# Attention's second score pass: the causal mask from coarse operand rows and GpSimd selects in place of mask matmuls

## The chip, the core and the metric

The kernel runs on one core of a Trainium2 chip. The metric is the device time of one execution in microseconds. A core has five engines: TensorE (PE; PEld is its weight load), VectorE (DVE), ScalarE (ACT), GpSimd (POOL) and SyncE (SP), which work in parallel, each in its own order, and wait for one another by semaphores. SyncE and ScalarE issue DMAs on hardware queues, GpSimd on a software one.

## The reference, cut to what matters

A two-layer transformer piece: causal attention with ALiBi, an expert-choice feed-forward layer, a gated scan mixer and a token-choice expert layer. The change lies in the first:

```python
x = x + _L0_attn_ref(_layernorm(x), W_attn, W_proj)   # x: 16 batches x 512 tokens x 128
# inside: H = 16 heads of D = 8
scores = einsum('bhqd,bhkd->bhqk', q, k) / sqrt(D)
bias   = where(k_pos <= q_pos, slope_h * (k_pos - q_pos), -inf)
att    = softmax(scores + bias, axis=-1)
y      = einsum('bhqk,bhkd->bhqd', att, v)
```

Every score with a key later than its query must add nothing to the softmax.

## The kernel before

**Attention** (function `attention`) takes the first 827 us. Its work is cut into 16 batches of 4 units; a unit is 4 heads of one batch. The scores are made twice. The first pass (S, lines 309 to 321) has queries on partitions and is only there for the row maxima, which VectorE reduces from PSUM (line 425). The second pass (E, lines 322 to 339) has keys on partitions and queries along the row; the maximum is already subtracted in it by two operand rows, and ScalarE takes the exponential (line 486) into `probs`. The products with V (line 344) sum over keys on TensorE.

Both passes contract over operand tiles `qop` and `kop` ([128, 16 heads, 512], bf16), of which there are two sets that alternate by batch. Rows 0 to 47 hold bf16 parts of q and k, rows 48 to 50 the ALiBi terms, rows 96 and 97 the maxima; all other rows are zero. S reads rows 0 to 95, E all 128. The constant rows are loaded once per set by `constant_rows` on SyncE, when VectorE has cleared the set (`s_init`); `s_rows[n]` counts them, and TensorE waits for it before a batch's first S.

**The mask.** A tile j of 128 keys needs the queries from 128 j on, and only its diagonal block of 128 x 128 holds pairs to be masked. Before each group of score matmuls a matmul of the identity with a constant tile of 0 and -1e30 writes this block: `maskq` in S (line 316), `maskk` in E:

```python
pe.matmul(out[:, :, 0:P], identb[:], maskk[:, 0:per, :], start=True, stop=False, ...)   # L332
for a in range(per):
    mm = pe.matmul(out[:, a, :], kop[...], qop[...], start=False, ...)                   # L335
```

A unit has 11 of these in E: eight of 128 columns, two of 256, one of 512.

**The order.** `ORDER` lists the pieces of a step by hand: S0 to S10 of unit u, E0 to E5 of unit u - 2, M (the maxima turned to rows), V0 and V1 of unit u - 2, V2 and V3 of unit u - 3. Four steps (st = 0 to 3) make a batch. SyncE writes the maximum rows into `qop` (line 194, two DMAs a unit); E0 waits for them.

**The next batch's operands** are made in between: statistics and normalisation on VectorE in step 0, x transposed after S5 of step 0, q projected at the end of step 0, k after S4 of step 1 and v at the end of step 2. For q and k in turn ScalarE takes the high part, VectorE the rest (line 395), GpSimd the middle and low parts (lines 257, 259) and sends them to DRAM (line 231); when both have landed, `place` on GpSimd issues six DMAs (lines 242, 244) that bring them back as operand rows. The next batch's S0 waits for these (`s_op`).

Of the kernel before, what the change touches and what calls it, by code (L numbers as in the profile page):

```python
# [14 lines left out]
BF16 = mybir.dt.bfloat16  # L15
# [3 lines left out]
ALU = mybir.AluOpType  # L19
# [3 lines left out]
P = 128  # L23
C = 128
T = 512
NB = 16
TT = T // P
# [4 lines left out]
H = 16  # L32
D = C // H
G = 4
HG = H // G

TERMS = [(0, 0), (1, 0), (2, 0), (0, 1), (1, 1), (0, 2)]
ROW_ALIBI = 8 * len(TERMS)
ROW_MAX = 96
# [21 lines left out]
def attention(nc, x_all, ident, x_in, w_attnT, qkv_scr, y_scr, rec_scr, shared, c_ident, c_identb, c_maskq, c_maskk, c_rows, nb=NB):  # L61


    with ExitStack() as ctx:
        def sb(name, shape, dt):
            return ctx.enter_context(nc.sbuf_tensor(name, shape, dt))

        def sem(name):
            return ctx.enter_context(nc.semaphore(name))
# [8 lines left out]
        maskk = sb("maskk", [P, HG, P], BF16)  # L78
# [43 lines left out]
        s_ex = sem("exp_done")  # L122
        s_pv = sem("pv_done")
# [3 lines left out]
        EN = 6  # L127
# [46 lines left out]
        def _(sp):  # L174
            for dst, src in ((x_all[:, 0:2 * TT, :], x_in[:, 0:2 * TT, :]), (ident[:], c_ident), (identb[:], c_identb),
                             (maskq[:], c_maskq), (maskk[:], c_maskk),
                             (wT[:], w_attnT.rearrange("c (s f) -> c s f", s=3))):
                sp.dma_start(dst, src).then_inc(s_first, 16)
            def constant_rows(n):
                sp.wait_ge(s_init[n], 2)  # L180
                for dst, a, b in ((kop[n][ROW_ALIBI:ROW_ALIBI + 3], 0, 3), (qop[n][ROW_ALIBI:ROW_ALIBI + 3], 3, 6),
                                  (kop[n][ROW_MAX:ROW_MAX + 2], 6, 8)):
                    sp.dma_start(dst.rearrange("p h q -> p (h q)"), c_rows[a:b]).then_inc(s_rows[n], 16)

# [30 lines left out]
        def _(pool):  # L215
# [32 lines left out]
            def prepare(n, b, first=False):  # L248
# [3 lines left out]
                if first:  # L252
                    clear_v(0)
                for s in range(2):

                    pool.wait_ge(s_mf, s + 2 if first else MISC0 + MISC * (b - 1) + 2 * s + 2)
                    pool.tensor_tensor(parts[s][:, 1], rest[:], zeros[:], ALU.add).then_inc(s_mid, 1)  # L257
                    pool.wait_ge(s_mid, 2 * b + s + 1)
                    pool.tensor_tensor(parts[s][:, 2], rest[:], parts[s][:, 1], ALU.subtract).then_inc(s_lo, 1)
                    keep_part(n, b, s)  # L260
                if b == 1:
                    pool.wait_ge(s_init[1], 2)
                place(n, b)

            prepare(0, 0, True)
            clear_v(1)
            for b in range(1, nb):
                prepare(b % 2, b)

        @block.tensor  # L270
        def _(pe):
            pe.wait_ge(s_first, 96)
# [24 lines left out]
            def step(n, b, st, last):  # L297
# [4 lines left out]
                    if st == 0 and there(G * b):  # L302
                        pe.wait_ge(s_op, 16 * 6 * (b + 1))
                        pe.wait_ge(s_rows[n], 48)
                    for what in ORDER:
# [16 lines left out]
                        if what[0] == "E" and there(u_exp):  # L322
                            j, h0, nh = e_units[k]
                            u = k
                            bank = psE[u % 2]
                            if k == 0:
                                pe.wait_ge(s_mrow, 32 * (u_exp + 1))
                            per = nh // 2 if j < 3 else 4
                            pe.wait_ge(s_ex, EN * u_exp + u)
                            for h in range(0, nh, per):  # L330
                                out = bank[:, h // per, 0:per * W[j]].rearrange("p (h q) -> p h q", h=per)
                                pe.matmul(out[:, :, 0:P], identb[:], maskk[:, 0:per, :], start=True, stop=False, skip_group_check=True)  # L332
                                for a in range(per):
                                    hh = HG * e + h0 + h + a
                                    mm = pe.matmul(out[:, a, :], kop[m][:, hh, P * j:P * j + P], qop[m][:, hh, P * j:T],  # L335
                                                   start=False, stop=(a == per - 1), skip_group_check=True)
                            mm.then_inc(s_er, 1)
                        u_v, m_v, e_v = (u_exp, m, e) if k < 2 else (u_exp - 1, m_old, e_old)
                        if what[0] == "V" and there(u_v):
                            pe.wait_ge(s_ex, 1 + EN * u_v + [2, 4, 5, 6][k])  # L340
# [22 lines left out]
        def _(dve):  # L363
# [22 lines left out]
            dve.wait_ge(s_first, 96)  # L386
# [1500 lines left out]
def two_blocks_kernel(nc, x, wattnT, wprojT, rw, rb, w1, b1, w2, b2, win, wout, prm, rows, gwT, rmsw, W1T, W2T, W3T, cst, out):  # L1887
# [13 lines left out]
    with ExitStack() as keep:  # L1901
# [5 lines left out]
        with ExitStack() as ctx:  # L1907
# [11 lines left out]
                      cst["c_maskq"], cst["c_maskk"], cst["c_rows"], nb)  # L1919
# [21 lines left out]
def constants(nt, bf16):  # L1941
# [8 lines left out]
    for _ in range(3):  # L1950
# [3 lines left out]
    rows += [np.ones((H, T), bf16)] * 3 + [-np.ones((H, T), bf16)] * 2  # L1954
    digits = np.array([[4.0 ** (7 - k) * j for j in (1, 1, 2, 3)] + [4.0 ** (7 - k) * 3 - 0.5] for k in range(9)])
    return dict(
        c_ident=np.eye(P, dtype=np.float32), c_identb=np.eye(P, dtype=np.float32).astype(bf16),
        c_maskq=wide(below[:, None], (P, HG, P), bf16), c_maskk=wide(below.T[:, None], (P, HG, P), bf16),
# [52 lines left out]
```

## Time and profile before

| | us |
|---|---|
| median of 3 runs | 1905.36 |
| the runs | 1899.95 to 1909.52 |
| the profiled execution | 1911.37 |
| its span | 1909.6 |
| TensorE, VectorE, ScalarE, GpSimd busy | 1386.0, 1278.0, 739.0, 817.9 |

All rows come from the profiled execution; their times count from the start of its span. "Busy" is the union of an engine's instructions. A matmul's duration includes its way through the array, so what one costs in a dense row of them is the distance between starts.

### The profile page before, as it was taken

To read this page: it belongs to the slowest core of one execution; us is meant where nothing else is said; L and a number is where in the kernel's file an instruction comes from. 1 tells how busy PE (TensorE), PEld (TensorE's weight loads), DVE (VectorE), ACT (ScalarE), POOL (GpSimd) and SP (SyncE) were. 2 spreads that over 40 slices of the span, in tenths; PEclk is the share of its full clock that TensorE was granted. 3 is DMA by queue.
4 is the path that set the end of the run, shared out by engine and by line. 5 is a ranking of instruction groups with operands and counts; after the bars stand their busy time and mean duration, and the time that the engine had idled before them with its cause. 6 is when DMAs were issued, how large, how long until landed. Compare 5 with 4: busy or idle time off the path is not lost. (4 is left out here: it accounts for less than half of the span.)

```text
span 1909.6 us, 33952 instructions
## 1 busy us (share of the span) xinstructions
PE 1386.0 (73%) x9370; PEld 869.1 (46%) x9371; DVE 1278.0 (67%) x3736; ACT 739.0 (39%) x1489; POOL 817.9 (43%) x716
## 2 busy tenths in 40 slices
PE   1788889889888988949315254541809999999996
PEld 0355445555555545438204222221806556555654
DVE  4667667667677766738671189998686666666664
ACT  0255445445555555511212132222424444444443
POOL 3222222222222222024006546565616888888886
PEclk9999899999999999965557765565559999999999
DMA  3533333233233233136104300030032333333332
GB/s 76 133 73 71 63 74 80 64 75 81 74 74 72 72 72 74 39 125 220 43 0 112 63 30 22 16 112 6 22 163 38 41 43 42 42 41 43 41 42 35
DMA packets 72986, 124.48 MB, mean 65 GB/s; under 512 B 17888, under 2 KB 42272, under 8 KB 70480
## 3 DMA queue, kind: packets, MB, share of 16 engines
q0 software_dynamic: 39168, 59.42, 18.6%
q1 hardware_dynamic: 25728, 51.42, 8.3%
q10 hardware_dynamic: 8032, 12.93, 1.9%
q8 instruction: 28, 0.46, 0.1%
q14 instruction: 30, 0.25, 0.1%
HBM read 65.25 MB, written 57.94 MB: 65 GB/s over the span
## 5 line engine op out<-in xcount | busy, mean ns | idle before, releaser
L425 DVE TENSOR_REDUCE mx<-psS 128x1 f32<-128x384 f32 (+3 forms) x704 | 428.2, 638 | 222.5 <-PE psS L319 211.9
L486 ACT ACTIVATE probs<-psE 128x1024 f32<-128x1024 f32 (+2 forms) x384 | 326.7, 884 | 290.3 <-PE psE L335 289.2
L316 PE MATMUL psS<-maskq,identb 128*128 128x128 bf16 (+2 forms) x704 | 178.5, 254 | 109.4 <-DMA kop<-qkv_scr 88.3
L1804 POOL DMA_INDIRECT out<-ex_y,ex_idx x144 | 235.8, 1638 | 48.6 <-issue 42.6
L319 PE MATMUL psS<-kop,qop 96*128 96x128 bf16 (+3 forms) x1024 | 246.5, 309 | 0.0
L335 PE MATMUL psE<-qop,kop 128*128 128x512 bf16 (+3 forms) x1024 | 231.4, 307 | 0.0
L332 PE MATMUL psE<-maskk,identb 128*128 128x128 bf16 (+2 forms) x704 | 175.0, 249 | 2.5 <-ACT probs L486 2.5
L344 PE MATMUL psY<-probs,vaug 128*32 128x512 f32 (+3 forms) x2048 | 176.5, 455 | 0.0
L1795 POOL DMA_INDIRECT ex_xg<-expert_tab,ex_idx x144 | 141.8, 985 | 66.2 <-issue 42.1
L316 PEld LDWEIGHTS psS<-maskq,identb 128*128 128x128 bf16 x704 | 67.8, 98 | 204.2 <-DVE mx L425 81.7
L1778 DVE SCALAR_TENSOR_TENSOR ex_h<-ex_psG,ex_w,ex_up 128x352 f32<-128x352 f32 x144 | 84.1, 584 | 109.9 <-ACT ex_w L1879 107.7
L257 POOL TENSOR_TENSOR parts<-rest,zeros 128x512 bf16<-128x512 f32 x32 | 40.7, 1272 | 261.7 <-DVE rest L395 261.5
L1862 PE MATMUL ex_psY<-ah_w3s,ex_hT 128*128 (+1 forms) x864 | 133.1, 290 | 0.7 <-ACT ex_hT L1873 0.7
L335 PEld LDWEIGHTS psE<-qop,kop 128*128 128x128 bf16 x1024 | 95.8, 99 | 59.3 <-issue 9.7
L251 POOL TENSOR_TENSOR rstd<-veps,mhalf 128x4 f32<-128x4 f32 x16 | 16.6, 1036 | 243.0 <-DVE veps L374 243.0
L1862 PEld LDWEIGHTS ex_psY<-ah_w3s,ex_hT 128*128 128x128 f32 (+1 forms) x864 | 107.7, 191 | 20.7 <-issue 2.7
L319 PEld LDWEIGHTS psS<-kop,qop 96*128 96x128 bf16 x1024 | 98.7, 101 | 36.0 <-issue 5.0
L1844 PE MATMUL ex_psU<-ah_w1s,ex_xT 128*128 x288 | 110.4, 465 | 0.5 <-ACT ex_xT L1883 0.5
L1845 PE MATMUL ex_psG<-ah_w2s,ex_xT 128*128 x288 | 109.8, 463 | 0.0
L1872 ACT ACTIVATE ex_hT<-ex_psH 128x256 f32<-128x256 f32 x144 | 55.2, 383 | 135.2 <-PE ex_psH L1838 135.2
L344 PEld LDWEIGHTS psY<-probs,vaug 128*32 128x32 f32 x2048 | 71.2, 114 | 59.7 <-issue 36.7
L1222 PE MATMUL mx_psO<-mx_wout,mx_z 128*128 128x128 f32 x128 | 33.0, 440 | 86.1 <-DVE mx_z L1362 86.1
(309 smaller groups left out, 2669.9 us busy)
## 6 DMA issues: line engine op xcount, KB each, us to landing
y_scr<-ysb SPq DMA_DIRECT2D x64, 256.0 KB, 2.2
qkv_scr<-parts POOLq DMA_DIRECT2D x32, 384.0 KB, 3.4
qop<-qkv_scr POOLq DMA_DIRECT2D x16, 384.0 KB, 5.8
kop<-qkv_scr POOLq DMA_DIRECT2D x16, 384.0 KB, 6.5
expert_tab<-table_rows SPq DMA_DIRECT2D x1, 4352.0 KB, 14.5
qop<-qkv_scr POOLq DMA_DIRECT2D x16, 256.0 KB, 7.2
kop<-qkv_scr POOLq DMA_DIRECT2D x16, 256.0 KB, 8.3
pj_num<-y_scr SPq DMA_DIRECT2D x16, 256.0 KB
```

What stands on the lines that cost most here:

```text
L316: pe.matmul(out[:, :, P * j:w], identb[:], maskq[:, 0:nh, :], start=True, stop=False, skip_group_check=True)
L319: mm = pe.matmul(out[:, h, :], qop[n][0:96, hh, P * j:P * j + P], kop[n][0:96, hh, 0:w], start=False, stop=(h == nh - 1), skip_group_check ...
L332: pe.matmul(out[:, :, 0:P], identb[:], maskk[:, 0:per, :], start=True, stop=False, skip_group_check=True)
L335: mm = pe.matmul(out[:, a, :], kop[m][:, hh, P * j:P * j + P], qop[m][:, hh, P * j:T], start=False, stop=(a == per - 1), skip_group_check= ...
L344: mm = pe.matmul(psY[32 * h:32 * h + 32, P * k:T], vaug[m_v][:, k, HG * e_v + h, :], probs[e_v % 2][k][:, h, :], start=(k == 0), stop=(k = ...
L425: dve.tensor_reduce(mx[:, j, h0:h0 + nh], psS[u % 2][:, 0:nh * w].rearrange("p (h k) -> p h k", h=nh), AX, ALU.max).then_inc(s_su, 1)
L486: act.activation(dst, src, ACT.Exp).then_inc(s_ex, 1)
L1795: pool.indirect_dma_start(xg[t % 4][:], None, ytab, bass.IndirectOffsetOnAxis(ap=idx[t % 8][:], axis=0))\
L1804: pool.indirect_dma_start(out, bass.IndirectOffsetOnAxis(ap=idx[t % 8][:], axis=0), y[m][:], None, compute_op=ALU.add).then_inc(s_sc[m], 16)
L1844: pe.matmul(psU[n][:, 0:DE], xT[n][:], flat(w1s[:, e, :]), start=True, stop=True).then_inc(s_g2, 1)
L1845: pe.matmul(psG[n][:, 0:DE], xT[n][:], flat(w2s[:, e, :]), start=True, stop=True).then_inc(s_g, 1)
L1862: i = pe.matmul(psY[:, 0:C], hT[m][0:wd, f], flat(w3s[0:wd, f, e, :]), start=(f == 0), stop=(f == len(FC) - 1))
```

## The change

The E pass no longer has its mask matmuls: the first score matmul of a bank has `start=True` itself. The mask comes in two parts. A coarse one is put into rows 51 to 81 of both operand sets, one row for each boundary between blocks of 16 positions: the `kop` row is 1 for keys in block i, the `qop` row -1e30 for queries in blocks before i. They work in both passes, and the S pass keeps `maskq` beside them. What is left, keys later than the query within the same block of 16, GpSimd sets to zero after the exponential, with one `affine_select` on the diagonal block of each `probs` tile: four a unit, 128 partitions x 4 heads x 128. The V matmuls wait for the selects (`s_msk`) and no longer for the exponential. GpSimd's work is written out anew, so that its selects stand among the preparation of the next batch. The 31 rows of each tile are loaded by one more DMA each on SyncE.

```diff
+ROW_SUB = ROW_ALIBI + 3
+SUB = 16
+NSUB = T // SUB - 1
...
-        maskk = sb("maskk", [P, HG, P], BF16)
...
+                for dst, a in ((kop[n], 0), (qop[n], NSUB)):
+                    sp.dma_start(dst[ROW_SUB:ROW_SUB + NSUB], c_subs[a:a + NSUB].unsqueeze(1).to_broadcast([NSUB, H, T]))\
+                        .then_inc(s_rows[n], 16)
...
+            def clear_future(u, j):
+                if 0 <= u < G * nb:
+                    pool.wait_ge(s_ex, 1 + EN * u + (2, 4, 5, 6)[j])
+                    block_ = probs[u % 2][j][:, :, 0:P]
+                    pool.affine_select(block_, block_, [[0, HG], [1, P]], ALU.is_ge, 0.0, base=0, channel_multiplier=-1).then_inc(s_msk, 1)
...
+            for b in range(nb + 1):
+                more = b + 1 < nb
+                for st in range(G if b < nb else 2):
+                    u = G * b + st - 2
+                    if st == 0 and more:
+                        factors(b + 1)
+                    if st == 1 and more:
+                        split_rest(b + 1, 0)
+                    if st == 2 and more:
+                        if b == 0:
+                            pool.wait_ge(s_init[1], 2)
+                        place(1 - b % 2, b + 1)
+                    for j in range(2):
+                        clear_future(u, j)
+                    if st == 1 and more:
+                        split_rest(b + 1, 1)
+                    for j in range(2, TT):
+                        clear_future(u, j)
...
-                        pe.wait_ge(s_rows[n], 48)
+                        pe.wait_ge(s_rows[n], 80)
...
-                                pe.matmul(out[:, :, 0:P], identb[:], maskk[:, 0:per, :], start=True, stop=False, skip_group_check=True)
...
-                                                   start=False, stop=(a == per - 1), skip_group_check=True)
+                                                   start=(a == 0), stop=(a == per - 1), skip_group_check=True)
...
-                            pe.wait_ge(s_ex, 1 + EN * u_v + [2, 4, 5, 6][k])
+                            pe.wait_ge(s_msk, TT * u_v + k + 1)
...
+    sub_of, sub = np.arange(T) // SUB, 1 + np.arange(NSUB)[:, None]
+    subs = np.concatenate([sub_of == sub, np.where(sub_of < sub, -1e30, 0.0)])
```

`factors` is the `rstd` power of line 251, `split_rest` lines 256 to 260 for q (s = 0) or k (s = 1).

SyncE's queue at the start, from the first constant rows to the first maximum rows. Before (names: tile written <- source, rows x elements):

```order
L183 DMA kop<-c_rows 3x8192
L183 DMA qop<-c_rows 3x8192
L183 DMA kop<-c_rows 2x8192
L183 DMA kop<-c_rows 3x8192
L183 DMA qop<-c_rows 3x8192
L183 DMA kop<-c_rows 2x8192
L194 DMA qop<-mT 1x4x512 x6
```

and now:

```order
L186 DMA kop<-c_rows 3x8192
L186 DMA qop<-c_rows 3x8192
L186 DMA kop<-c_rows 2x8192
L188 DMA kop<-c_subs 31x16x512
L188 DMA qop<-c_subs 31x16x512
L186 DMA kop<-c_rows 3x8192
L186 DMA qop<-c_rows 3x8192
L186 DMA kop<-c_rows 2x8192
L188 DMA kop<-c_subs 31x16x512
L188 DMA qop<-c_subs 31x16x512
L200 DMA qop<-mT 1x4x512 x6
```

In each set, two DMAs of 31 rows x 16 heads x 512 stand behind the three small ones, and set 1's stand ahead of the first maximum rows.

TensorE in a step, from E2 to S5 (psE is E's PSUM tile, psS is S's). Before:

```order
L332 MATMUL psE<-maskk,identb 128x128
L335 MATMUL psE<-qop,kop 128x384
L332 MATMUL psE<-maskk,identb 128x128
L335 MATMUL psE<-qop,kop 128x384
L316 MATMUL psS<-maskq,identb 128x128
L319 MATMUL psS<-kop,qop 128x384
L332 MATMUL psE<-maskk,identb 128x128
L335 MATMUL psE<-qop,kop 128x384
L332 MATMUL psE<-maskk,identb 128x128
L335 MATMUL psE<-qop,kop 128x384
L316 MATMUL psS<-maskq,identb 128x128
L319 MATMUL psS<-kop,qop 128x384
```

and now:

```order
L363 MATMUL psE<-qop,kop 128x384 x2
L345 MATMUL psS<-maskq,identb 128x128
L348 MATMUL psS<-kop,qop 128x384
L363 MATMUL psE<-qop,kop 128x384 x2
L345 MATMUL psS<-maskq,identb 128x128
L348 MATMUL psS<-kop,qop 128x384
```

The matmuls of `maskk` are gone; nothing else has moved.

GpSimd while it prepares a batch. Before, from `rstd` into the six operand DMAs (parts: the three parts of q or k; qkv_scr: their copy in DRAM):

```order
L251 TENSOR_TENSOR rstd<-veps,mhalf 128x4
L257 TENSOR_TENSOR parts<-rest,zeros 128x512
L259 TENSOR_TENSOR parts<-rest,parts 128x512
L231 DMA qkv_scr<-parts 128x3x512
L257 TENSOR_TENSOR parts<-rest,zeros 128x512
L259 TENSOR_TENSOR parts<-rest,parts 128x512
L231 DMA qkv_scr<-parts 128x3x512
L242 DMA qop<-qkv_scr 24x8192
L244 DMA kop<-qkv_scr 24x1x8192
```

and now, the part of steps 1 and 2 of a batch:

```order
L262 TENSOR_TENSOR parts<-rest,zeros 128x512
L264 TENSOR_TENSOR parts<-rest,parts 128x512
L237 DMA qkv_scr<-parts 128x3x512
L272 AFFINE_SELECT probs_0<-probs_0 128x4x128
L272 AFFINE_SELECT probs_1<-probs_1 128x4x128
L262 TENSOR_TENSOR parts<-rest,zeros 128x512
L264 TENSOR_TENSOR parts<-rest,parts 128x512
L237 DMA qkv_scr<-parts 128x3x512
L272 AFFINE_SELECT probs_2<-probs_2 128x4x128
L272 AFFINE_SELECT probs_3<-probs_3 128x512
L248 DMA qop<-qkv_scr 24x8192
L250 DMA kop<-qkv_scr 24x1x8192
```

Two selects now stand between the splitting of q and of k, two between k's DMA to DRAM and the operand DMAs, and the next unit's selects behind those.

## Rows read from the trace of the kernel before

**Rows 1.** Busy time by windows: attention's batches 1 to 14, then batch 15 and the end.
```profile
99.20:762.20 663.00, 591.65 (x5265) 337.82 (x5266) 462.72 (x998) 337.43 (x448) 149.61 (x181) 0.95 0.32 73
762.20:827.00 64.80, 52.93 (x498) 28.24 (x498) 36.42 (x58) 33.32 (x43) 0.10 (x1) 0.95 0.16 52
```

**Rows 2.** Timeline, TensorE: first score matmul of batches 1, 8 and 9 (start, us).
```profile
99.22 0.61 PE L316 MATMUL psS<-maskq,identb 128*128 128x512 bf16 x1 [8.97 <-DMA kop<-qkv_scr]
...
434.85 0.39 PE L316 MATMUL psS<-maskq,identb 128*128 128x512 bf16 x1 [1.20 <-DMA kop<-qkv_scr]
...
482.05 0.39 PE L316 MATMUL psS<-maskq,identb 128*128 128x512 bf16 x1 [4.09 <-DMA kop<-qkv_scr]
```

**Rows 3.** Timeline, TensorE, one step: mask matmuls (L332) and what follows each.
```profile
450.55 0.22 PE L332 MATMUL psE<-maskk,identb 128*128 128x128 bf16 x1
450.61 0.32 PE L335 MATMUL psE<-qop,kop 128*128 128x384 bf16 x1
...
453.25 0.27 PE L332 MATMUL psE<-maskk,identb 128*128 128x256 bf16 x1
453.36 0.38 PE L335 MATMUL psE<-qop,kop 128*128 128x256 bf16 x2
...
454.18 0.38 PE L332 MATMUL psE<-maskk,identb 128*128 128x512 bf16 x1
454.40 0.39 PE L335 MATMUL psE<-qop,kop 128*128 128x128 bf16 x4
```

**Rows 4.** Timeline, TensorE: S4 of the same batch's step 0; V2 and V3 of step 2.
```profile
440.46 0.23 PE L316 MATMUL psS<-maskq,identb 128*128 128x128 bf16 x1 [1.11 <-DVE mx L425]
...
459.66 0.81 PE L344 MATMUL psY<-probs,vaug 128*32 128x256 f32 x13
```

**Rows 5.** Timeline, GpSimd: preparing batch 9's operands during batch 8.
```profile
448.50 1.28 POOL L257 TENSOR_TENSOR parts<-rest,zeros 128x512 bf16<-128x512 f32 x1 [10.18 <-DVE rest L395]
...
451.58 0.82 POOL L231 DMA_DIRECT2D qkv_scr<-parts  x1 [0.57 <-POOL parts L259]
454.94 1.27 POOL L257 TENSOR_TENSOR parts<-rest,zeros 128x512 bf16<-128x512 f32 x1 [2.54 <-DVE rest L395]
...
457.74 0.79 POOL L231 DMA_DIRECT2D qkv_scr<-parts  x1 [0.30 <-POOL parts L259]
461.03 0.55 POOL L242 DMA_DIRECT2D qop<-qkv_scr  x1 [2.50 <-DMA qkv_scr<-parts]
```

**Rows 6.** Timeline, ScalarE: exponentials of E3 in that step 1.
```profile
453.06 0.81 ACT L486 ACTIVATE probs<-psE 128x768 f32<-128x768 f32 x1
```

**Rows 7.** Groups by form, GpSimd (last two numbers before the bar: busy us, mean ns).
```profile
L257 POOL TENSOR_TENSOR parts<-rest,zeros 128x512 bf16<-128x512 f32 x32 | 40.7, 1272 | 261.7 <-DVE rest L395 261.5
...
L1449 POOL TENSOR_TENSOR gt_scaled<-x_all,gt_acc_a 128x512 f32<-128x512 f32 x8 | 8.3, 1039 | 0.6
...
L217 POOL MEMSET zeros<- 128x512 f32 x1 | 0.5, 527 | 0.0
```

**Rows 8.** Timeline, SyncE: the constant rows of operand set 0.
```profile
9.44 0.32 SPq L183 DMA_DIRECT2D kop<-c_rows  x1
9.80 0.24 SPq L183 DMA_DIRECT2D qop<-c_rows  x1
```

**Rows 9.** DMA view, 9.3 to 16 us in 40 slices, and SyncE's queue (packets, MB, share).
```profile
GB/s 0 0 0 0 0 0 293 0 0 0 0 0 294 0 0 0 0 0 0 0 0 0 0 196 0 0 0 0 0 0 0 0 0 0 0 0 0 0 0 0
...
q1 hardware_dynamic: 16, 0.13, 10.5%
```

**Rows 10.** DMA view, 822.1 to 824.1 us: SyncE's queue under the projection's loads.
```profile
q1 hardware_dynamic: 159, 0.29, 48.0%
```

**Rows 11.** DMA view, 394.9 to 396.1 us: SyncE's queue, two DMAs of maximum rows.
```profile
q1 hardware_dynamic: 16, 0.01, 2.3%
```

**Rows 12.** Timeline, TensorE, batch 0: its first score matmul; first exponent matmul of unit 0.
```profile
51.24 0.61 PE L316 MATMUL psS<-maskq,identb 128*128 128x512 bf16 x1 [25.62 <-DMA kop<-qkv_scr]
...
71.80 0.38 PE L335 MATMUL psE<-qop,kop 128*128 128x512 bf16 x1
```

More of the change, by code:

```diff
@@ L58, in kept_sums, with attention @@
     return y_scr[lo:hi, :, D, :]
-def attention(nc, x_all, ident, x_in, w_attnT, qkv_scr, y_scr, rec_scr, shared, c_ident, c_identb, c_maskq, c_maskk, c_rows, nb=NB):
+def attention(nc, x_all, ident, x_in, w_attnT, qkv_scr, y_scr, rec_scr, shared, c_ident, c_identb, c_maskq, c_rows, c_subs, nb=NB):
     with ExitStack() as ctx:
@@ L122, in attention @@
         s_ex = sem("exp_done")
+        s_msk = sem("future_cleared")
         s_pv = sem("pv_done")
@@ L175, in _ @@
             for dst, src in ((x_all[:, 0:2 * TT, :], x_in[:, 0:2 * TT, :]), (ident[:], c_ident), (identb[:], c_identb),
-                             (maskq[:], c_maskq), (maskk[:], c_maskk),
+                             (maskq[:], c_maskq),
                              (wT[:], w_attnT.rearrange("c (s f) -> c s f", s=3))):
@@ L246, in place, with factors @@
                     row += w
-            def prepare(n, b, first=False):
+            def factors(b):
                 pool.wait_ge(s_xn, b)
@@ L251, in prepare @@
                 pool.tensor_tensor(rstd[:], veps[:], mhalf[:], ALU.pow).then_inc(s_rstd, 1)
[L252 to L265, printed above, removed]
-            clear_v(1)
-            for b in range(1, nb):
-                prepare(b % 2, b)
+            def split_rest(b, s):
+                pool.wait_ge(s_mf, MISC0 + MISC * (b - 1) + 2 * s + 2 if b else s + 2)
+                pool.tensor_tensor(parts[s][:, 1], rest[:], zeros[:], ALU.add).then_inc(s_mid, 1)
+                pool.wait_ge(s_mid, 2 * b + s + 1)
+                pool.tensor_tensor(parts[s][:, 2], rest[:], parts[s][:, 1], ALU.subtract).then_inc(s_lo, 1)
+                keep_part(b % 2, b, s)
@@ new lines, in clear_future @@
+            def clear_future(u, j):
[3 more added lines that the diff above has]
+                    pool.affine_select(block_, block_, [[0, HG], [1, P]], ALU.is_ge, 0.0, base=0, channel_multiplier=-1).then_inc(s_msk, 1)
+            factors(0)
+            clear_v(0)
+            for s in range(2):
+                split_rest(0, s)
+            place(0, 0)
+            clear_v(1)
@@ L270, in _ @@
         @block.tensor
         def _(pe):
-            pe.wait_ge(s_first, 96)
+            pe.wait_ge(s_first, 80)
             def x_transposes(b, use):
@@ L385, in _ @@
             dve.memset(kop[0][:].bitcast(F32), 0.0).then_inc(s_init[0], 1)
-            dve.wait_ge(s_first, 96)
+            dve.wait_ge(s_first, 80)
             norm_stats(0)
@@ L1918, in two_blocks_kernel @@
             attention(nc, x_all, ident, x, wattnT, qkv_scr, y_scr, rec_scr, shared, cst["c_ident"], cst["c_identb"],
[L1919 removed]
+                      cst["c_maskq"], cst["c_rows"], cst["c_subs"], nb)
             project(nc, x_all, y_scr, rec_scr, shared, wprojT, x_scr, rw, rb, norm_tab, score_tab, scores, ident, nb)
@@ L1957, in constants @@
         c_ident=np.eye(P, dtype=np.float32), c_identb=np.eye(P, dtype=np.float32).astype(bf16),
-        c_maskq=wide(below[:, None], (P, HG, P), bf16), c_maskk=wide(below.T[:, None], (P, HG, P), bf16),
+        c_maskq=wide(below[:, None], (P, HG, P), bf16),
+        c_subs=subs.astype(bf16),
         c_rows=np.stack(rows).reshape(8, H * T),
```

## The prediction

> **What bounds the kernel now.** I read the windows first. Batches 1 to 14 of attention take 663.0 us, 47.4 us each, with TensorE busy for 591.65 us of them [rows 1]. So TensorE looks like the bound, and mask matmuls taken from it look like time won. The timeline says otherwise. Every batch opens with TensorE idle for its operand rows to come back from DRAM: 15 such waits after batch 0's, from 1.20 to 8.97 us [rows 2]. A batch is therefore a loop: first score matmul, k's projection in step 1, the split on VectorE and GpSimd, a round trip through DRAM, the next first score matmul. What TensorE saves between k's projection and the batch's end only lengthens the wait. The third thing to read is the start of the kernel, where SyncE loads the constant rows [rows 8, 9], for the change puts four large DMAs there.
>
> **What the change removes.** In a dense row of matmuls, the one behind a mask matmul starts 0.06 us after it for 128 columns, 0.11 for 256 and 0.22 for 512 [rows 3]. A unit has 8, 2 and 1 of them: 0.48 + 0.22 + 0.22 = 0.92 us, or 59 us for 64 units. Of this only what lies on the loop counts. In step 0, S4 waits 1.11 us for VectorE [rows 4], which normalises the next batch there; what E0 to E3 save ahead of or near it is lost in this wait but for some 0.06 us. E4 and E5 behind it give 0.44. In step 1 the masks of E0 to E3 stand ahead of S6, behind which VectorE splits k: 8 x 0.06 = 0.48. Together 1.0 us a batch. The other 2.6 us of a batch's four units go into the wait for the operands (4.09 us in batch 9 [rows 2]).
>
> **What it adds on GpSimd.** Four selects a unit, 512 elements a partition, in and out of SBUF. The trace has no select. Below, the nearest row is a memset of this size, 0.53 us, which only writes; above, the two-input addition, 1.27 us; another two-input product takes 1.04 [rows 7]. I take 1.0 us: one input, but a comparison with it. The Trainium skill (GPSIMD Engine Reference, Performance pitfalls for Q7 kernels) gives compare-and-select bodies 1.03 to 2.03 cycles an element, from which I estimate 0.44 to 0.87 us at its 1.2 GHz; no row here shows it, and it would leave the sum as it is.
>
> Where they stand in the queue matters more. In step 1, q's DMA to DRAM is issued until 452.40 us, k's split began at 454.94, and E3's exponential ended at 453.87 [rows 5, 6]. The select of probs_0 fits in at 452.4. That of probs_1 must wait for E3's exponential and ends at about 454.9: k's split starts 0.1 us late at 1.0 us a select, 0.3 at 1.27. The next two selects stand between k's DMA to DRAM (done at 458.53) and the operand DMAs (461.03), where GpSimd waited 2.50 us for the landing [rows 5]: two selects fit up to 1.25 us each. V2 and V3 of the next step stood at 459.66 [rows 4]; their selects end at about 460.6, so TensorE stalls for some 1 us there, and again before V0, since the six operand DMAs (3.3 us) go first. These stalls come after k's projection; the wait for the operands hides them, with 4.09 + 2.6 us of cover. If that cover were gone, they would cost some 2 us a batch. ScalarE and VectorE issue what they did.
>
> So a batch gains 1.0 - 0.1 = 0.9 us, 14 of them 12.6. Batch 15 has no operands to wait for: 4 x 0.92 = 3.7 us, less two selects (2.0) behind the last exponential: 1.7. Sum of the steady part: **-14 us**. The clock there was 0.95 of full [rows 1]; the waits stay about as long, so I leave it alone.
>
> **What it adds at the start.** Each of the four new DMAs carries 31 rows x 16 KB = 508 KB, in pieces of 1 KB. Which engines carry it decides the case. The small DMAs of 3, 3 and 2 rows were issued within 0.7 us [rows 8], but their bytes stand in three separate slices, at 10.3, 11.3 and 13.2 us, with nothing else moving [rows 9]: each row went to an engine of its own, and the next DMA's rows queued on the same engines, in order. The projection's loads, whose outermost dimension is 8, kept 48.0% of 16 engines busy, at most eight [rows 10]. The number of engines follows the outermost dimension; 31 has no divisor up to 16 but 1, and I take **one engine**. The Trainium skill (DMA: Bandwidth & Descriptors, Why a DMA increments its semaphore by 16 and not by 1) says this outright: the largest count up to 16 that divides the slowest dimension of both sides, on the lowest-numbered engines. By that rule 31 rows go to one engine, and the trace agrees for 3 rows and for 8.
>
> An engine's rate: 0.29 MB in 0.480 x 16 x 2.0 = 15.4 engine-us is 19 GB/s with 2 KB packets [rows 10]; 8 KB in 0.023 x 16 x 1.2 = 0.44 engine-us is 19 GB/s with 1 KB packets [rows 11]. The lower bound is 0.13 MB in 0.105 x 16 x 6.7 = 11.3 engine-us, 11.5 GB/s [rows 9]. I take 19, since those packets are the nearest in size: 26.7 us a DMA. Set 0's two start at about 14.4 us (13.2 plus a row) and set 1's follow on the same engine, ahead of unit 0's maximum rows, which share that queue. Four make 107 us. I add 10 us for this engine's sixteenth of the operand rows of batches 0 and 1 (2 x 1.5 MB / 16 at 19 GB/s). The queue is empty at 131 us.
>
> Three waits follow. S0 of batch 0, at 51.24 us [rows 12], needs set 0's rows, at about 73. E0 of unit 0, at 71.80 [rows 12], needs the maximum rows: 131. Batch 1's S0 needs set 1's rows: 131 too. The second rules: from 71.80 to TensorE's arrival at batch 1 (99.22 - 8.97 = 90.25 [rows 2]) it had 18.4 us of work, now 16.6 without the masks of two units, and arrives at 148. Batch 1's operands have landed by then, its 8.97 us of waiting are used up, and the cost is 148 - 99 = **+49 us**. The mask tile that is no longer loaded saves nothing, as the clearing of the operand sets outlasts it.
>
> **Sum.** 49 - 14 = +35. The profiled execution took 1911.37 us (span 1909.6), which gives 1946; it stands 6.0 us above the median, and from the median 1905.36 the time is **1940 us**.
>
> **Rivals.**
> - A, the forecast: 1940. With 22 GB/s (packets without their gaps) the queue is empty at about 115: 1924; some more traffic on the engine: 1955. Chance 0.57.
> - B, the 31 rows are spread over many engines. Four times 0.5 MB are then in before 51.24 us, as the 0.29 MB of [rows 10] were within 2 us on eight engines. Nothing is left at the start but the -14: 1905 - 14 = 1891, faster. It decides as soon as set 0's rows land by 51 us and set 1's by 70, which three engines do. For it speaks that the loads in the trace with few rows had 16 or fewer; against it the separate slices of [rows 9]. [...] Chance 0.14.
> - C, one engine, but the maximum rows do not queue behind. Then batch 1's S0 waits for set 1's rows alone: 131 - 99 = +32, less 14: 1923. Chance 0.10.
> - D, selects of 2 us (GpSimd's software being slow, as nothing here excludes): k's split starts 1.5 us late, the operand DMAs another 1.5, so each batch grows by 2 us instead of shrinking: +28, the end 0, the start +49: 1982. The gain is gone at about 1.5 us a select. Chance 0.13.
> - E, one engine at 11.5 GB/s: 44 us a DMA, queue empty at 207, start +125: 2016. Chance 0.06.
>
> **The numbers.** The range 1903 to 1985 holds A, C and D and leaves out B and E, 0.20; A's own range is 1920 to 1960. A measurement of this kernel tells about 0.5%, 9.5 us, from no change: 1896 to 1915. Faster comes from B (0.12); the same from what is left of B (0.02) and the low ends of A and C (0.04 each): 0.10; slower is the rest, 0.78.
>
> **What would show it.** At the start: E0 of unit 0 at 110 to 150 us instead of 71.80, waiting for a DMA; S0 of batch 0 at 65 to 80; long stretches with a DMA share of 1/16. From batch 1 to 15: 46.5 us a batch instead of 47.4; waits for kop<-qkv_scr still at every batch start; k's split within 0.3 us of the exponential-plus-select; selects of 0.8 to 1.3 us; TensorE waiting about 1 us for GpSimd in step 2 and hardly elsewhere. It is wrong if E0 of unit 0 stands near 70 us (then B), if GpSimd is busy through the batch (D), or if the operand waits vanish, for then the 59 us were all to be had.

## The result and the profile after

The change makes the kernel slower: 1963.31 us (median of four runs, 1961.09 to 1974.93) against 1907.44 us for the kernel before (four runs, 1899.95 to 1911.22), a ratio of 1.031 with a 95% interval of 1.026 to 1.036. That lies inside the forecast's range of 1903 to 1985, 23 us above its 1940 and 3 above the 1960 at which the range of its case A ended. The profiled execution took 1962.95 us, its span is 1961.2 us and its mean granted clock 0.835, against 1909.6 us and 0.842 before.

The windows of the changed kernel, cut as in [rows 1] at the first score matmul (S0) of batch 1 and of batch 15 (window, length, then busy us and count of TensorE, its weight load, VectorE, ScalarE and GpSimd, granted clock, DMA share, GB/s); the second window ends at the projection's first matmul:

```profile
166.20:817.80 651.60, 547.74 (x4649) 289.29 (x4650) 472.59 (x1011) 336.02 (x448) 289.70 (x406) 0.96 0.33 74
817.80:886.30 68.50, 48.05 (x433) 23.21 (x433) 36.14 (x58) 33.32 (x43) 16.30 (x26) 0.90 0.18 57
```

Batches 1 to 14 take 651.6 us, 11 less than the 663.0 of [rows 1]. TensorE's busy time fell by 44 us there, so three quarters of what it saved became idle time. From S0 of batch 15 to the projection's first matmul it is 68.5 us where the same stretch took 70.6 before. Both are gains. The loss is all ahead of the first window, which begins 67 us later than before (99.22 in [rows 2]). The timeline of TensorE there, with the start of batch 0, of unit 0's exponents and of batch 1:

```profile
75.77 0.59 PE L345 MATMUL psS<-maskq,identb 128*128 128x512 bf16 x1 [50.08 <-issue]
...
146.28 1.03 PE L363 MATMUL psE<-qop,kop 128*128 128x512 bf16 x2 [49.88 <-DMA qop<-mT]
...
166.19 0.38 PE L345 MATMUL psS<-maskq,identb 128*128 128x512 bf16 x1 [0.60 <-DVE mx L453]
```

S0 of batch 0 is 24.5 us later than in [rows 12], E0 of unit 0 waits 49.88 us for its maximum rows and is 74.5 us later, and batch 1 starts without waiting for operands. SyncE's own queue shows why the maximum rows are late (start, duration of the issue):

```profile
10.46 0.26 SPq L188 DMA_DIRECT2D kop<-c_subs  x1
10.75 22.78 SPq L188 DMA_DIRECT2D qop<-c_subs  x1
33.58 36.38 SPq L186 DMA_DIRECT2D kop<-c_rows  x1
...
70.61 0.26 SPq L188 DMA_DIRECT2D kop<-c_subs  x1
70.91 45.72 SPq L188 DMA_DIRECT2D qop<-c_subs  x1
116.68 24.15 SPq L200 DMA_DIRECT2D qop<-mT  x2
```

DMA issues that otherwise take about 0.26 us take 22.78, 36.38 and 45.72 us behind the 31-row loads, and SyncE issues nothing meanwhile. (With 32-row loads, in e1 below, the issues of `qop<-c_subs` take 0.49 us each.) The DMA view says how fast they go. First SyncE's queue from 56 to 67 us, when nothing else moves, and from 55 to 75 us, then from 33.6 to 53 us, while batch 0's operand rows are loaded, then from 86 to 118 us, while x and batch 1's operand rows are (packets, MB, share of 16 engines):

```profile
q1 hardware_dynamic: 246, 0.25, 6.8%
...
q1 hardware_dynamic: 457, 0.54, 8.5%
...
q1 hardware_dynamic: 114, 0.12, 3.4%
...
q1 hardware_dynamic: 227, 0.23, 3.2%
```

A share of 6.8% is about one engine of 16 (the 8.5% hold the small rows of set 1 too). Where nothing else moves, the view shows 22 to 26 GB/s in slice after slice, 23 on average, which is 45 ns for a piece of 1 KB. Under other traffic 0.12 MB take 19.4 us and 0.23 MB take 32, some 6 to 7 GB/s. The 1984 pieces of the four loads need 89 us undisturbed; they ran from 14.6 to 145.4 us, 42 us longer.

In the steady part, the waits of TensorE from 100 to 750 us (what waits for what: us in total, times, longest), before:

```profile
PE psS L316 <- DMA kop<-qkv_scr: 49.9, 13, 6.6
PE psS L316 <- DVE mx L425: 8.2, 15, 1.1
PE psM L355 <- DVE rest L395: 2.5, 14, 0.2
```

and after:

```profile
PE psE L363 <- DMA qop<-mT: 59.3, 7, 49.9
PE psS L345 <- DMA kop<-qkv_scr: 44.2, 11, 7.7
PE psS L345 <- DVE mx L453: 24.1, 66, 1.6
PE psY L372 <- POOL probs L272: 4.5, 13, 1.0
```

The operand waits are still there, as the forecast said; VectorE is now waited for 66 times in place of 15; the selects cost few direct waits. One wait is new and was not foreseen: apart from the 49.9 us at the start, E0 waits six times later on, up to 2.71 us, for maximum rows, where before no such wait stands in the list. It goes with the selects: it is 12.0 us in e1 below and 0.2 in e4, which leaves them out. The groups by form give a select's price (busy us, mean ns), which no row of before had:

```profile
L272 POOL TENSOR_SCALAR_AFFINE_SELECT probs<-probs 128x512 f32<-128x512 f32 x256 | 158.5, 639 | 320.0 <-ACT probs L514 319.6
```

It is 0.64 us. GpSimd's timeline during batch 2, against [rows 5]:

```profile
232.29 0.63 POOL L272 TENSOR_SCALAR_AFFINE_SELECT probs<-probs 128x512 f32<-128x512 f32 x1 [0.73 <-ACT probs L514]
233.18 1.28 POOL L262 TENSOR_TENSOR parts<-rest,zeros 128x512 bf16<-128x512 f32 x1 [0.25 <-DVE rest L423]
...
236.79 1.22 POOL L272 TENSOR_SCALAR_AFFINE_SELECT probs<-probs 128x512 f32<-128x512 f32 x2
239.28 0.56 POOL L248 DMA_DIRECT2D qop<-qkv_scr  x1 [1.26 <-DMA qkv_scr<-parts]
```

k's split waits 0.25 us for VectorE's remainder and not for the select ahead of it. The next two selects fit into the wait for the landing, of which 1.26 us are left.

### The profile page after: what moved, and what is told of

It is laid out like the page before. It is cut to its first block and busy times, and to the rows that moved or that the text cites. A ratio compares the mean times of both kernels' runs of the same rounds, so it can differ in the third digit from the quotient of the medians.

```text
span 1961.2 us, 32900 instructions
## 1 busy us (share of the span) xinstructions
PE 1336.4 (68%) x8666; PEld 813.4 (41%) x8667; DVE 1283.6 (65%) x3736; ACT 737.7 (38%) x1489; POOL 976.9 (50%) x972
## 3 DMA queue, kind: packets, MB, share of 16 engines
q0 software_dynamic: 39168, 59.42, 17.9%
## 5 line engine op out<-in xcount | busy, mean ns | idle before, releaser
L272 POOL TENSOR_SCALAR_AFFINE_SELECT probs<-probs 128x512 f32<-128x512 f32 x256 | 158.5, 639 | 320.0 <-ACT probs L514 319.6
L363 PE MATMUL psE<-qop,kop 128*128 128x512 bf16 (+3 forms) x1024 | 212.7, 311 | 62.5 <-DMA qop<-mT 59.3
L363 PEld LDWEIGHTS psE<-qop,kop 128*128 128x128 bf16 x1024 | 89.8, 99 | 111.1 <-DMA qop<-mT 50.2
L1208 POOL TENSOR_TENSOR mx_rstd<-mx_nrm_veps,mx_mhalf 128x8 f32<-128x8 f32 (+1 forms) x19 | 40.7, 2142 | 92.9 <-DVE mx_nrm_veps L595 84.0
```

Of the source, the lines that this page charges most:

```text
L272: pool.affine_select(block_, block_, [[0, HG], [1, P]], ALU.is_ge, 0.0, base=0, channel_multiplier=-1).then_inc(s_msk, 1)
```

## The experiments

Each was timed beside the kernel before, in five sessions: e1, e2, e4 and e5 (its median there 1907.47 us), e3 and e6 (1908.83), e7 and e8 (1903.61), e9 and e10 (1910.62), e11 (1905.78). Between sessions a difference of a few us says nothing. A window or a step length comes from one execution of each kernel. "Batches 1 to 14" is S0 of batch 1 to S0 of batch 15 in the profiled execution. In e1, e3, e4, e5, e7, e8 and e9 a 32nd coarse row of zeros goes with the 31, which changes no score.

### e1: 32 rows in place of 31

```
+ NROW = NSUB + 1
- dst[ROW_SUB:ROW_SUB + NSUB], c_subs[a:a + NSUB].unsqueeze(1).to_broadcast([NSUB, H, T])
+ dst[ROW_SUB:ROW_SUB + NROW], c_subs[a:a + NROW].unsqueeze(1).to_broadcast([NROW, H, T])
```

> The changed kernel with a 32nd coarse row of zeros, so that each new load has an outermost dimension of 32 instead of 31. Theory (31 rows run on one DMA engine, and set 1's rows and the maximum rows queue there): the queue at the start is gone, S0 of batch 0 near 51 us, E0 of unit 0 near 72 instead of 146, S0 of batch 1 near 99 instead of 166, time 1963 - 67 = 1896 us (1888 to 1902). Rival (the 2 MB themselves cost, however they are spread): E0 of unit 0 after 100 us, time above 1925.

Measured 1904.84 us, ratio 0.9995 (0.9971 to 1.0018). S0 of batch 0 is at 53.91 us, E0 of unit 0 at 74.36, and batch 1's first score matmul at 102.07, 2.5 us later than before (99.61) in place of 67. One row more takes 58 us off. From 10 to 20 us, while set 0's two loads are under way, SyncE's queue shows

```profile
q1 hardware_dynamic: 1060, 1.17, 71.0%
```

against the 6.8% of the change: the 32 rows are spread over most of the 16 engines. The start is settled: the cost is that 31 rows go one piece after another. The time is 3 us above the range given, because the gain of the steady part was half of what was expected: batches 1 to 14 took 656.9 us, 6.0 less than before.

### e2: the kernel before with the four loads alone

```
+ for dst, a in ((kop[n], 0), (qop[n], NSUB)):
+     sp.dma_start(dst[ROW_SUB:ROW_SUB + NSUB], c_subs[a:a + NSUB]...).then_inc(s_rows[n], 16)
- pe.wait_ge(s_rows[n], 48)
+ pe.wait_ge(s_rows[n], 80)
```

> The kernel before, with its mask matmuls, plus only the four 31-row loads. Theory: the whole start cost comes without the rest of the change: E0 of unit 0 near 146 us, time 1907 + 67 = 1974 us (1966 to 1981). Rival (the start is late because of GpSimd's new order or the missing mask tile): 1905 to 1915 us.

Measured 1978.07 us, ratio 1.0351 (1.0326 to 1.0375). Without any of the change's compute the four loads cost 70.6 us; the rest of the change is then worth 1978.07 - 1963.31 = 14.8 us, the 14 of the forecast's sum.

### e3: 31 rows for operand set 0, 32 for set 1

```
+ m = NROW if n else NSUB
```

> The change, with the coarse rows of operand set 0 loaded as 31 rows (on one DMA engine) and those of set 1 as 32 rows, the last one zero (on all). Theory (four loads on one engine's ring, in order; the second set is only late because it stands behind the first there, and because 16 KB operand rows and 1 KB rows take turns on that engine): the first S0 stays where the change has it, at 75 to 77 us; the wait for the maximum rows before the first E0 (49.88 us in the change) goes nearly away, so the first E0 is at 95 to 105 us and S0 of batch 1 at 115 to 125 us in place of 166.19. The total is 1911 to 1925 us, 38 to 52 below the change. Rival (what is late is SP's own queue, whatever the second set does): the first E0 stays behind 130 us and the total over 1945 us.

Measured 1932.54 us, ratio 1.012 (1.0068 to 1.0172), 31 below the change and 8 above the range given. The mechanism is the theory's: no wait for the maximum rows stands in TensorE's waits there, E0 of unit 0 is at 100.78 us in place of 146.28 and S0 of batch 1 at 127.73 in place of 166.19. But S0 of batch 0 is at 79.78 us, 3 later than the theory had it, and S0 of batch 1 is 3 later too. Part of that is given back in batches 1 to 14, which took 659.0 us. Set 0's loads are worth 1932.54 - 1904.84 = 28 us, set 1's the other 31.

### e4: e1 without the selects

```
- if 0 <= u < G * nb:                      + if False:
- pe.wait_ge(s_msk, TT * u_v + k + 1)      + pe.wait_ge(s_ex, 1 + EN * u_v + [2, 4, 5, 6][k])
```

> e1 without the 256 selects; the V matmuls wait for the exponentials again, and keys later than the query within a block of 16 stay in the sums (left out: that part of the mask). Theory (the selects lie in GpSimd's gaps and under the operand waits): within 5 us of e1, 1 to 2 us of that at attention's end. Rival (the selects delay k's split or the operand DMAs in each batch, or V on TensorE on the loop): 10 us or more faster than e1.

Measured 1899.03 us, ratio 0.9954 (0.9936 to 0.9972). The 256 selects cost 5.8 us here by the medians and 6.7 in batches 1 to 14, just over the 5 expected at most and well under the rival's 10; the two ratios' intervals touch. Batches 1 to 14 took 650.2 us: the masks' 59 us of TensorE are worth 12.7 us of the loop (forecast: 14 x 1.0). Its operand waits grew to 83.4 us from 100 to 750 us, where e1 has 55.1: that is where the rest of the saved time stands.

### e5 and e6: the operand rows in another order, with and without mask matmuls

```
- qkv_scr[n, 0, 0:k].rearrange("a (d h) q -> (a d) (h q)", d=D)
+ qkv_scr[n, 0, 0:k].rearrange("a (d h) q -> d a (h q)", d=D)
- k_src.unsqueeze(0).to_broadcast([k, D, H * T])
+ k_src.unsqueeze(1).to_broadcast([D, k, H * T])
```

e5 is e1 with this edit; e6 is the kernel before, its mask matmuls kept, with it.

> e1 with the operand rows in another order, d outermost and the part inside it, so that each of the six operand DMAs has an outermost dimension of 8, where kop's had 3 and 2. Theory (a batch is a loop through the operand round trip, whose last landing is set by the few engines of kop's DMAs): the operand waits of some 4 us a batch shrink to under 1, batch period 46.5 to 43.5 us, time 1896 - 14 x 3 = 1854 us (1845 to 1870). Rival (the round trip is bound by bytes or by the written partitions): landing unchanged, 1890 to 1900 us.

> The kernel before, mask matmuls kept, with only the order of the operand rows in the six operand transfers changed (outermost dimension of 8 in place of 2 and 3). Theory (before, each batch is a loop through the operand rows' transfer, and without that wait the steps are set by TensorE and VectorE together, so that the mask matmuls are only partly paid): batches 1 to 14 fall from 662.9 us to about 625 to 645 us (e5, without mask matmuls: 616.9), and the total is 1863 to 1888 us. Rival 1 (the mask matmuls cost their whole 0.92 us a unit once the wait is gone, 3.7 us a batch): batches 1 to 14 take 669 us or more, the total is 1905 to 1916 us, and the new order alone is worth nothing. Rival 2 (VectorE sets the steps, the mask matmuls are free): within 5 us of e5, 1852 to 1862 us.

e5 took 1857.09 us, ratio 0.9732 (0.9712 to 0.9752); e6 took 1854.67 us, ratio 0.9719 (0.967 to 0.9769). The wait that bounded each batch is gone in both. From 380 to 470 us, the last two operand transfers of each batch land (bytes, median us to landing) in e1 after

```profile
qop<-qkv_scr POOLq DMA_DIRECT2D x2, 128.0 KB, 15.6
kop<-qkv_scr POOLq DMA_DIRECT2D x2, 128.0 KB, 17.9
```

and in e5 after

```profile
qop<-qkv_scr POOLq DMA_DIRECT2D x2, 128.0 KB, 12.0
kop<-qkv_scr POOLq DMA_DIRECT2D x2, 128.0 KB, 13.1
```

The five microseconds between 17.9 and 13.1 are about what S0 waited for. The second result is the surprise: with the loop gone, the whole change (e5) is no faster than the kernel before with the same edit (e6). My theory (masks partly paid) and the rival (masks wholly paid) for e6 both fell, and its rival 2, within 5 us of e5, came out in the number. Its reason did not; e7 shows that.

### e7: e5 without the selects

The edit is that of e4.

> e5 (the change with a 32nd zero coarse row and with the operand rows in the new order) without GpSimd's selects; the output leaves out the mask inside the 16x16 blocks on the diagonal. Theory: with no operand wait in the loop, a step is set by VectorE's reductions and TensorE together; of e5's waits only those for POOL (7.3 us in 650) and part of those for the maximum rows hang on the selects, so the total falls by 3 to 8 us, to 1849 to 1854 us. Rival (the selects also slow VectorE, and so every step, since its hi/lo subtraction is 307 ns in e5 and 175 ns in e6, and its scalar operation 390 against 328): VectorE's groups go back to their times of before and the total falls by 10 to 20 us, to 1837 to 1847 us.

Measured 1826.39 us, ratio 0.9592 (0.957 to 0.9613): 31 us below e5 and 28 below e6, in other sessions; by the ratios it is 27 and 24, and the profiles have the projection's first matmul 29.3 and 31.1 us earlier. So selects and mask matmuls cost some 24 to 31 us each here; that they are equal is chance. Neither the theory nor the rival had it so large. The windows over batches 1 to 14 of e5, e6 and e7, in this order:

```profile
93.60:710.40 616.80, 536.35 (x4592) 284.70 (x4648) 471.35 (x1009) 339.97 (x448) 292.49 (x406) 0.98 0.37 79
```
```profile
90.20:709.30 619.10, 572.80 (x5181) 325.74 (x5264) 460.51 (x1002) 339.60 (x448) 152.46 (x182) 0.99 0.37 78
```
```profile
92.60:682.00 589.40, 532.11 (x4650) 283.70 (x4649) 458.44 (x996) 338.64 (x448) 152.23 (x182) 0.99 0.39 82
```

e5 and e7 run the same matmuls; e5 needs 27.4 us more for its 14 batches, 2.0 a batch. Three things are seen. VectorE is 12.9 us busier. TensorE waits 7.3 us for GpSimd from 100 to 700 us and 3.0 for maximum rows, neither of which e7 has; e7 in turn waits 7.9 us for operand rows again, in six short waits. And the granted clock is 0.98 in place of 0.99. Here is VectorE's subtraction for the maximum rows beside GpSimd's selects in e5:

```profile
338.24 0.69 DVE L464 TENSOR_TENSOR mhl<-mx,mhl 128x16 bf16<-128x16 f32 x1
```
```profile
338.24 1.22 POOL L273 TENSOR_SCALAR_AFFINE_SELECT probs<-probs 128x512 f32<-128x512 f32 x2
```

and the same step in e7:

```profile
325.48 0.18 DVE L464 TENSOR_TENSOR mhl<-mx,mhl 128x16 bf16<-128x16 f32 x1
```

0.69 us in place of 0.18, at the head of the chain that leads to the maximum rows. Over 100 to 700 us its mean is 307 ns in e5 and 175 in e7. The Trainium skill (SBUF — State Buffer, SBUF: two separate sides) says that a VectorE operation with two SBUF inputs and a GpSimd operation that reads SBUF exclude each other for a whole instruction; these rows agree. The normalising scalar operation (`xn`) takes 387 ns in e5 and 328 in e7; no run shows why.

The clock falls in step 0, behind a wait of the same length in both. e5:

```profile
319.40 0.29 PE L346 MATMUL psS<-maskq,identb 128*128 128x128 bf16 x1 [1.22 <-DVE mx L454]
319.48 0.53 PE L349 MATMUL psS<-kop,qop 96*128 96x384 bf16 x1
319.80 0.85 PE L364 MATMUL psE<-qop,kop 128*128 128x384 bf16 x2
```

e7:

```profile
308.17 0.23 PE L346 MATMUL psS<-maskq,identb 128*128 128x128 bf16 x1 [1.22 <-DVE mx L454]
308.24 0.33 PE L349 MATMUL psS<-kop,qop 96*128 96x384 bf16 x1
308.40 0.49 PE L364 MATMUL psE<-qop,kop 128*128 128x384 bf16 x2
```

The same matmuls take 0.53 and 0.85 us at the lower level (1.2 GHz, granted clock 0.53 from 319.40 to 322.80 us) and 0.33 and 0.49 at the higher one. The falls can be counted by the windows of step 0. Batches 8 and 9 of e5:

```profile
401.89:415.60 13.71, 11.61 (x84) 6.12 (x85) 9.97 (x29) 6.27 (x8) 3.54 (x5) 0.88 0.05 20
447.13:459.12 11.99, 10.00 (x84) 5.19 (x85) 10.30 (x29) 6.16 (x8) 3.67 (x5) 1.00 0.06 23
```

In nine of e5's 14 batches the clock falls and step 0 takes 13.47 to 13.73 us; in the other five it takes 11.78 to 12.11: 1.6 us a fall. e7 has four. e11 below runs the same matmuls and selects as e5 and has four falls as well: its batches 1 to 14 take 609.9 us, 7.0 less than e5's and 20.5 more than e7's. So of the 27.4 us some 7 go with the clock and some 20 with the selects. What makes it fall in one batch and not in the next is not shown.

### e8: e5 with the mask matmuls back in step 0

```
+ if st == 0:
+     pe.matmul(out[:, :, 0:P], identb[:], maskk[:, 0:per, :], start=True, stop=False, ...)
- start=(a == 0)
+ start=(a == 0 and st > 0)
```

> e5 with the kernel before's mask matmuls put back in step 0 of each batch alone (the step in which VectorE also makes the next batch's norms, and in which the granted clock of e5 falls to the lower level for some 3.5 us after TensorE's waits for VectorE; in e6, with all mask matmuls, it does not fall). Theory (without mask matmuls TensorE idles enough in step 0 to lose its clock, which gives back what their leaving saves): the granted clock of 100 to 700 us rises from 0.97 to 0.99 or 1.00, batches 1 to 14 fall from 616.9 to 590 to 608 us, and the total is 1835 to 1848 us, below both e5 and e6. Rival (VectorE sets the steps whatever TensorE does): the total is within 4 us of e5, 1853 to 1861 us, even where the clock rises.

Measured 1856.81 us, ratio 0.975 (0.9728 to 0.9771): as e5. The rival held: step 0 took 13.04 us, e5's 13.03, and batches 1 to 14 took 622.2 us. Its reason did not: the clock falls in five batches in place of e5's nine, some 6 us less by 1.6 a fall (an estimate), and where it holds, step 0 takes 12.3 to 13.0 us where e5's takes 11.8 to 12.1. So the equal time hides two changes that about cancel: what the clock gave back, the mask matmuls cost. The expectation's remark that in e6 the clock does not fall was wrong too: it falls there in batches 1 and 8.

### e9: selects in step 3 alone, mask matmuls in steps 0 to 2

```
+ if st != 3:
+     pe.matmul(out[:, :, 0:P], identb[:], maskk[:, 0:per, :], start=True, stop=False, ...)
+ for j in range(2 if st == 3 else 0): clear_future(u, j)
+ for j in range(2, TT if st == 3 else 2): clear_future(u, j)
```

> The mask matmuls of the kernel before in the exponentials' units of steps 0, 1 and 2 of each batch, GpSimd's selects in those of step 3 alone, operand rows in the new order of e5 and e6. Mean step lengths so far: e6 (all masks) 12.46, 11.06, 10.48, 10.22 us for steps 0 to 3; e5 (all selects) 13.03, 10.66, 10.64, 9.74; e7 (neither) 11.82, 10.56, 9.82, 9.89. Theory (what a mask matmul or a select costs is paid in the step in which it runs): step 3 falls to about 9.7 us, the others stay as in e6, so a batch takes 43.5 to 43.9 us in place of 44.22 and the total is 1844 to 1852 us. Rival (the selects' late halves fall into step 0 and lengthen it by the 0.6 us that e5 has there over e6): nothing is left, 1853 to 1861 us.

Measured 1847.99 us, ratio 0.9659 (0.9619 to 0.9698), the fastest version that computes everything, 63 us below the kernel before in its session. Step 3 is 9.57 us, step 0 12.80 and the others as in e6: 0.65 less in step 3 (the theory had 0.5), and 0.34 more in step 0, of the rival's 0.6. Those 0.34 are the clock: step 0 has three more falls than in e6, of 1.6 us each, and in the other batches it is as long as there. Against e6 the 6.7 us are more than the 4.4 between the profiles (614.7 and 619.1 us), and the two ratios' intervals overlap; that e9 beats both kernels is sure, that it beats e6 is likely.

### e10: the table in memory two rows larger

```
- subs = np.concatenate([sub_of == sub, np.where(sub_of < sub, -1e30, 0.0)])
+ subs = np.concatenate([sub_of == sub, zero_row, np.where(sub_of < sub, -1e30, 0.0), zero_row])
```

> The change with only the table of coarse rows in memory grown from 62 to 64 rows (two zero rows that nothing loads); all four loads still take 31 rows. It tells whether the 5 us by which batches 1 to 14 of e1 and e3 (656.9 and 659.0 us) are slower than those of the change (651.6) come from where the tables lie in memory. If so: 656 to 660 us for these batches and a total of 1967 to 1971 us. Rival (they come from the 32-row loads or from when the loads end): 650 to 653 us and 1961 to 1965 us.

Measured 1966.02 us, ratio 1.0288 (1.0243 to 1.0333); batches 1 to 14 took 649.0 us. By the window the place of the tables is not the cause of e1's 5 us; the total lies between the two ranges and decides nothing. The kernels with 32 rows for set 1 have the lower granted clock in these batches (e1 and e3 0.94, the change and e10 0.96), as e5 (0.98) has against e11 (0.99). So the 5 us may be the clock's; what sets it is open.

### e11: the change with 31 rows and the new order of the operand rows

The edit is that of e5, on the change.

> The change, its four loads of 31 rows kept, with only the order of the operand rows changed as in e5 (outermost dimension of 8 in place of 3, 2 and 1). It tells why the coarse rows' 1984 pieces took from 14.6 to 145.4 us, 42 us more than at their undisturbed pace (45 ns each, 89 us). Theory (half of the operand rows go by the engine that also carries the coarse rows, and the two queues take turns there, a 16 KB row for a 1 KB piece; with eight engines it is an eighth): the pieces lose at most some 15 us, the first E0 (146.28 us in the change) is at 115 to 128 us and S0 of batch 1 (166.19) at 134 to 148 us. With e5's steady part the total is 1896 to 1912 us. Rival (the loads of x and the traffic of all engines slow the pieces, whatever the order of the operand rows): the first E0 stays at 140 to 148 us and the total is 1922 to 1932 us.

Measured 1926.84 us, ratio 1.0121 (1.0078 to 1.0164). The rival's numbers held: E0 of unit 0 is at 145.85 us and S0 of batch 1 at 165.28, as in the change. Its cause, the loads of x and the traffic of all engines, was not tested by itself. SyncE's queue from 33.6 to 53 us moved

```profile
q1 hardware_dynamic: 151, 0.15, 3.4%
```

some more than the 114 packets of the change, and from 86 to 118 us 196 against 227, although the operand transfers now have an outermost dimension of 8. How they are laid out is not why the coarse rows are slow beside them.

The lengths of the steps, as means over batches 1 to 14 (start of a step's first score matmul, behind its mask matmul, to the next one's; step 3 holds the wait for the operands), put the experiments side by side:

| kernel | step 0 | 1 | 2 | 3 | batch | time |
|---|---|---|---|---|---|---|
| before | 12.27 | 11.06 | 10.48 | 13.53 | 47.34 | 1907.44 |
| change | 11.67 | 10.64 | 10.51 | 13.73 | 46.55 | 1963.31 |
| e1: 32 rows | 11.81 | 10.64 | 10.52 | 13.95 | 46.92 | 1904.84 |
| e4: e1, no selects | 11.63 | 10.57 | 9.82 | 14.42 | 46.44 | 1899.03 |
| e6: before, new order | 12.46 | 11.06 | 10.48 | 10.22 | 44.22 | 1854.67 |
| e5: e1, new order | 13.03 | 10.66 | 10.64 | 9.74 | 44.07 | 1857.09 |
| e7: e5, no selects | 11.82 | 10.56 | 9.82 | 9.89 | 42.10 | 1826.39 |
| e9: selects in step 3 | 12.80 | 11.06 | 10.49 | 9.57 | 43.91 | 1847.99 |
| e11: change, new order | 12.50 | 10.66 | 10.65 | 9.75 | 43.57 | 1926.84 |

## Why the prediction was right, and where its sizes were off

**The bound.** Right. Each batch is a loop through the operand rows' transfer: all masks and selects gone save 0.9 us of the loop (e4) while their TensorE time goes into longer operand waits, and shortening the transfer saves 48 us (e1 to e5). The forecast's warning, that the operand waits vanishing would mean "the 59 us were all to be had", was wrong: with the waits gone in e6 and all but 7.9 us of them in e7, the masks are worth 24 to 31 us, since TensorE then waits for VectorE instead (42.2 us in e7, 31.1 in e6, from 100 to 700 us).

**The masks, 1.0 us a batch.** Right: 0.42 in step 1 (forecast 0.48), 0.60 in step 0 (0.50), in the change with its selects; in e4, without them, 0.49 and 0.64.

**The selects.** They were sized at 1.0 us, with 0.8 to 1.3 as the sign, and measured 0.64, inside the 0.44 to 0.87 that the forecast had estimated beside its sum and not used; and they fit where the order of GpSimd's queue had said. The forecast charged the selects 0.1 us a batch, by way of k's split. That way is free (k's split waits for VectorE), but e1 against e4 has 6.7 us in 14 batches, 0.5 each. They take 0.70 us of step 2 (10.52 in e1, 9.82 in e4), and the wait in step 3 gives back only 0.47 of it (13.95 and 14.42); steps 0 and 1 add 0.25. The cover is not whole. The warning that they would cost some 2 us a batch if the cover were gone came out in the number (e5 less e7, 2.0 a batch) by luck: only a quarter of it is the stall named, GpSimd awaited before V (0.5 a batch), and another quarter goes with the clock. The rest is not split by any run; VectorE's longer operations (0.9 a batch), which the forecast had issuing "what they did" and did not slow, are the part that is seen.

**The steady sum, -14.** Measured -11.3 for batches 1 to 14 and -2.1 for the end by the profiles; 14.8 by e2. Right. The same edits gave only 5.1 us once the start was mended (2.6 by e1's median against before, and 2.5 of e1's later start). e10 speaks against the place in memory; the granted clock was lower in e1 (0.94 against 0.96), and why stays open.

**The start, +49.** The mechanism was right in each link: one engine, the rows in order, the maximum rows behind them and E0 the wait that rules (e3 takes 31 us away by mending set 1 alone). The size was not: +67 by the profile, 70.6 by e2. The queue was empty at 145.4 us in place of 131, and from E0 of unit 0 to S0 of batch 1 TensorE took 19.9 us in place of the 16.6 forecast, the first 6.3 of them at the lower clock behind its wait of 49.88 us (granted clock 0.53 from 146.28 to 152.60 us; before, that stretch ran at 1.00). The rate was sized at 19 GB/s and measured 23, which by itself makes the four loads 89 us in place of 107. **The failed term is "I add 10 us" for other traffic**, a sixteenth of the operand rows by bytes. It measured 42: under other traffic the queue fell to between a quarter and a third of its pace, while batch 0's operand rows moved and again while x and batch 1's operand rows did, and x's loads were not in the term at all. A share by bytes was the wrong measure. That the total still came within 23 us is partly luck: the rate was 18 us too slow and the traffic term 32 too small. My own repair, that the operand rows crowd that one engine, fell with e11. Why the pieces are so slow beside other traffic stays open. The Trainium skill (DMA: Bandwidth & Descriptors, Queues, rings and completion order) has each engine serve its queues in turn, one packet at a time, a packet there being a group of some 9 to 17 descriptors; the trace does not name the engine that carries a piece, so no run here shows it.

**Rival B** decided by the number of rows alone: 32 rows behave nearly as it said, with S0 of batch 0 at 53.91 us, but then the change takes 1904.84 us and not B's 1891, no faster and no slower than the kernel before. **C** (the maximum rows not behind the coarse rows), **D** (slow selects) and **E** (11.5 GB/s) did not occur.

## What to carry to other kernels

Look at the outermost dimension of a broadcast or gathered load before its bytes: one row more (31 to 32) was worth 58 us here, and another order of the operand rows 48. When a wait bounds a loop, work taken from the busiest engine is nearly free of effect, and work added elsewhere looks free too; both prices appear only once the wait is gone (24 to 31 us each), so measure a trade of one engine's work against another's after the wait is mended, and with neither side in. GpSimd's work is not off the path because it is off TensorE: here VectorE's work took longer beside it (12.9 us over 14 batches), and TensorE was waiting for VectorE. And when two profiles differ by a few us, look at the granted clock step by step first: here one fall of it cost 1.6 us, and its number changed from kernel to kernel with the same matmuls.

## What the runs showed of the hardware that was not expected

- An issue of a DMA held SyncE for 22.78, 36.38 and 45.72 us behind 31-row loads of 496 pieces of 1 KB each; later, unrelated transfers on SyncE's queue (the maximum rows) waited with it.
- A stream of 1 KB pieces at a share of 6.8% of 16 engines ran at 23 GB/s alone and at 6 to 7 beside other traffic, and no better on the whole when the operand rows of that traffic were laid out in another order (e11).
- GpSimd's select over 512 fp32 elements a partition takes 0.64 us, half of its two-input addition (1.28).
- A VectorE subtraction of 16 elements a partition took 0.69 us beside a select and 0.18 without.
- Behind waits of the same 1.22 us TensorE's clock fell to the lower level (1.2 GHz, 0.53 granted over 3.4 us) in one kernel and not in the other, and in nine of e5's 14 batches but not in five: 1.6 us each.
